# Second sequence's causal triangle: zeroed in the exponentials by POOL and VectorE instead of masked by TensorE products

## The chip, the cores and the metric

The kernel runs on one core of one Trainium2 chip. The metric is the device time of one execution in microseconds (us). Engines are called by the profile's names: PE is TensorE, ACT ScalarE, DVE VectorE, POOL GpSimd, and SP starts most DMAs.

## What is computed

Two sequences of 512 rows by 128 features go through a cross attention, a block of causal self attention and a mixture of four experts, a second cross attention, and a small feed-forward net. The change touches the causal self attention alone:

```python
scores = jnp.einsum('bqhd,bkhd->bhqk', q, k) / jnp.sqrt(jnp.float32(D))
causal = jnp.tril(jnp.ones((T, T), dtype=bool))
scores = jnp.where(causal, scores, jnp.float32(-1e+30))
p = jax.nn.softmax(scores, axis=-1)
y = jnp.einsum('bhqk,bkhd->bqhd', p, v).reshape(B, T, C)
```

There are 16 heads of 8 features (T is 512, B is 2 here). Weights of keys that lie after the query must come out as zero.

## The kernel before

The self attention runs in 32 steps s, 16 for each sequence (s = 0 to 15 the first, 16 to 31 the second). A step is four heads and one tile of 128 keys (kt = s % 4), against all queries from that tile on, so its width w is 512, 384, 256 and 128 columns for kt 0 to 3. The heads of a step are handled as pair 0 and pair 1. In a step, in this order on their engines:

- PE computes the scores of pair 0 and of pair 1, transposed (keys on partitions), into PSUM banks 0 to 3. Each pair waits for the exponential of the same pair in step s - 1, which frees its banks (`st_exp`).
- ACT takes the exponential of each pair into the SBUF buffer `PTb`, which has room for two steps: it waits until PE has used what was written two steps before (`av_step`).
- PE computes `outputs(s - 1)` (four products with the values, 32 columns of weights each) after the scores of step s. It reads `PTb`.
- In steps up to 21 PE also computes three "ring" scores each step, of which DVE takes the row maxima (`ring_maximum`, line 882, tile `mB`); two banks are used in turn, so PE and DVE wait for each other there.

Only the first 128 columns of a step lie across the diagonal and need the triangle set to nothing. In the first sequence POOL does it in the exponentials (an affine select, two heads at a time, semaphore `st_masked`, line 606). In the second sequence PE adds a constant -1e30 triangle to the scores: a product of the identity `identb` with `mask_kq`, of tile `cstb`, behind each of the four score products of a step.

The queues are in the order in which the code is written; nothing reorders them. Work of other stages is put between the steps at fixed step numbers. Those that matter here:

- DVE: `copy_outputs` (line 890) empties the bank in which the outputs of four steps gather; it stands first in step s when s % 4 is 1, and PE's first `outputs` of the next four steps waits for it (`yg_ready`). `normalise_group` follows at s % 4 == 2. `add_attention` and `ln_m` are at step 20, `route(0)` (lines 937 to 951) at step 23, `weigh_last` (lines 983, 984, nine instructions) at step 24, `place_rows(0)` (lines 958 to 977) at step 25.
- POOL: `split_maxima(c)` (lines 566 to 572) splits the maxima of a chunk of heads; PE's `turn_maxima(c)` and the later steps' scores wait for it. Chunk 7 is split after `ln_rsqrt("m")` (line 516) and `apply_m(0)` (line 616) of the next stage, and PE turns it at the end of step 23. Then POOL scatters the rows to the experts' slots, as soon as `place_rows(0)` is done.
- PE: `turn_normalised(0)` at step 18, `project_outputs(0)` at 19, `turn_sums(0)` at 21, `logits(0)` at 22, `rank_rows(0)` at 24, a product for `cb_mm` at 26. After step 31: `outputs(31)`, `turn_slots(0, ...)` and the experts' products.
- ACT: steps 27 to 31 also carry `load_experts(0)` and `copy_weights` of the first experts (0.6 us each).

Of the kernel before, what the change touches and what calls it, by code (L numbers as in the profile page):

```python
# [23 lines left out]
ALU = mybir.AluOpType  # L24
# [3 lines left out]
P = 128  # L28
B, T, D = 2, 512, 128
# [18 lines left out]
LEAST = -3.0e38  # L48
# [45 lines left out]
def program(nc, t_in, out):  # L94
    ctx = ExitStack()
    with ctx:
        def sb(name, shape, dt=F32):
            return ctx.enter_context(nc.sbuf_tensor(name, shape, dt))

        def sem(name):  # L100
            return ctx.enter_context(nc.semaphore(name))
# [10 lines left out]
        cst = sb("cst", [P, 3, P])  # L112
# [16 lines left out]
        mB = sb("mB", [P, B, HB, QT])  # L129
        mp = sb("mp", [P, 2, 3, HG * QT], BF16)  # L130
        mr = sb("mr", [P, HG * QT])
        nm3 = sb("nm3", [3 * HG * QT, 2, P], BF16)
        rB = sb("rB", [P, 2, HB])
        lg = sb("lg", [P, 4, NT, E])
# [181 lines left out]
        stack_ready = [[sem(f"stack_ready{b}_{g}") for g in range(HB // HG)] for b in range(B)]  # L316
        ones_ready = sem("ones_ready")
        s_mm, s_max = sem("s_mm"), sem("s_max")
        s1_mm, s1_max = sem("s1_mm"), sem("s1_max")
        m_part, m_turned, m_copied = sem("m_part"), sem("m_turned"), sem("m_copied")  # L320
        m_ready = [sem(f"m_ready{r}") for r in range(2)]
# [52 lines left out]
        M_CHUNK = 2 * HG  # L374
        N_CHUNK = B * HB // HG
        S_CHUNK = (None, 0, 3, 7, 11, 15, 20, 23)
        S_SPLIT = {2: 2, 6: 3, 10: 4, 14: 5}
        S_VAUG = 2
        S_TAIL = 18
        S_LN = 21  # L380
# [31 lines left out]
            return 6 if part else LN_BANK  # L412

        ident = cst[:, 0, :]
        identb, mask_qk, mask_kq = cstb[:, 0, :], cstb[:, 1, :], cstb[:, 2, :]
        block = ctx.enter_context(nc.Block())


# [83 lines left out]
        def _(pool):  # L502
# [53 lines left out]
            def split_maxima(c):  # L556

                b, g = divmod(c, HB // HG)
                m = mB[:, b, HG * g:HG * g + HG, :].rearrange("p h t -> p (h t)")
                pool.wait_ge(s_max, min(M_CHUNK * (c + 1), M0))  # L560
                if c >= 2:
                    pool.wait_ge(s1_max, ring_done(c))
                    pool.wait_ge(m_turned, c - 1)
                if c:
                    pool.wait_ge(m_part, 3 * c)
                pool.tensor_copy(mp[:, c % 2, 0], m).then_inc(m_part, 1)
                pool.wait_ge(m_part, 3 * c + 1)
                pool.tensor_tensor(mr[:], m, mp[:, c % 2, 0], ALU.subtract).then_inc(part_step, 1)
                pool.wait_ge(part_step, c + 2)
                pool.tensor_copy(mp[:, c % 2, 1], mr[:]).then_inc(m_part, 1)  # L570
                pool.wait_ge(m_part, 3 * c + 2)
                pool.tensor_tensor(mp[:, c % 2, 2], mr[:], mp[:, c % 2, 1], ALU.subtract).then_inc(m_part, 1)
# [26 lines left out]
                    pool.indirect_dma_start(XN[:, QT * b + t, :], None, scr_y[b],  # L599
                                            bass.IndirectOffsetOnAxis(ap=pos[:, b, t:t + 1], axis=0)).then_inc(gathered[b], 16)  # L600

            for n in range(2 * 16):
                s, pair = divmod(n, 2)
                slot = 4 * ((s + 1) % 2) + 2 * pair
                pool.wait_ge(st_exp, n + 1)
                pool.affine_select(PTb[:, slot:slot + 2, 0:P], PTb[:, slot:slot + 2, 0:P], [[0, 2], [1, P]], ALU.is_ge, 0.0,  # L606
                                   base=0, channel_multiplier=-1).then_inc(st_masked, 1)
                if pair and s in S_SPLIT:
                    split_maxima(S_SPLIT[s])
            split_maxima(6)  # L610

            def apply_m(b):
                pool.wait_ge(ln_rstd["m"], b + 1)
# [33 lines left out]
        def _(dve):  # L647
# [146 lines left out]
                dve.tensor_copy(cstb[:], cst[:]).then_inc(consts_ready, 1)  # L794

            def row_biases():
                own(dve.tensor_copy(rowbias[:], maskx[:]))
                own.wait()
                own(dve.tensor_scalar(rowbias[:], rowbias[:], -1.0, 1.0, ALU.mult, ALU.add))
                own.wait()  # L800
                own(dve.tensor_scalar(rowbias[:], rowbias[:], -MASK_NEG, None, ALU.mult))
# [210 lines left out]

            for m in range(M0):
                maximum(m)
            for s in range(2 * 16):
                g = (s - 5) // QT
                if s % QT == 1 and s >= 5:
                    copy_outputs(*divmod(g, 4))
                if s < M_STEPS:
                    ring_maximum(3 * s)  # L1020
                if s % QT == 2 and s >= 6 and not 4 <= g < 5:
                    normalise_group(*divmod(g, 4))
                if s == 1:
                    weigh_router()
                elif s == 3:
                    centre_router()
                elif s == S_TAIL + 2:
                    add_attention(0)
                    ln_m(0)
                elif s == S_TAIL + 5:  # L1030
                    route(0)
                    normalise_group(1, 0)
                elif s == S_RANK:
                    weigh_last()
                elif s == S_RANK + 1:
                    place_rows(0)
                elif s == S_CB + 1:
                    bias_last()
                if s < M_STEPS:
                    ring_maximum(3 * s + 1)  # L1040
                    ring_maximum(3 * s + 2)
            copy_outputs(1, 3)
            normalise_group(1, 3)
            add_attention(1)
# [331 lines left out]
        def _(pe):  # L1376
            def mm(o, lhsT, rhs, start=True, stop=True):
                return pe.matmul(o, lhsT, rhs, start=start, stop=stop)  # L1378
# [285 lines left out]
            def outputs(s):  # L1664

                bg, kt = divmod(s, QT)
                b, g = divmod(bg, 4)
                if s < 16:
                    pe.wait_ge(st_masked, 2 * s + 2)
                else:  # L1670
                    pe.wait_ge(st_exp, 2 * s + 2)
                if s == 0:
                    pe.wait_ge(v_ready, 3)
                    pe.wait_ge(preC_act, N_PREC)
                elif s == 16:
                    pe.wait_ge(v_ready, 3 * B)

                if kt == 0 and bg:
                    pe.wait_ge(yg_ready, bg)
                for j in range(4):  # L1680
                    i = mm(PS[32 * j:32 * j + 32, AV_BANK, kt * P:T], vaug[:, b, kt, 4 * g + j, :],
                           PTb[:, 4 * ((s + 1) % 2) + j, 0:T - kt * P], start=kt == 0, stop=kt == QT - 1)
                i.then_inc(av_step, 1)
# [79 lines left out]
            for s in range(2 * 16):  # L1763
# [7 lines left out]
                for pair in range(2):  # L1771
                    if s >= 1:
                        pe.wait_ge(st_exp, 2 * (s - 1) + pair + 1)
                    else:
                        pe.wait_ge(s_max, M0 - 2 + pair)
                    for j in range(2):
                        h = 4 * g + 2 * pair + j
                        o = PS[:, 2 * pair + j, 0:w]
                        i = mm(o, ks[b][:, h, kt * P:kt * P + P], qs[b][:, h, kt * P:T], stop=b == 0)
                        if b:  # L1780
                            i = mm(o[:, 0:P], identb, mask_kq, start=False)
                    i.then_inc(st_mm, 1)
                    if s < M_STEPS:
                        ring_scores(3 * s + pair)
# [225 lines left out]
```

## Time and profile before

| | |
|---|---|
| time, median of 3 runs | 346.1 us (345.12 to 346.39) |
| the profiled execution's own time | 344.6 us |
| its span in the trace | 342.7 us |
| PE busy | 319.4 us, 93% of the span |
| DVE busy | 240.8 us, 70% |
| ACT busy | 216.5 us, 63% |
| POOL busy | 127.6 us, 37% |

The page of the profile gives each engine's busy time, the granted clock of PE, and the chain of work that ended last, of which 64% lies on PE. Busy times of PE overlap, since its products are pipelined: what one costs in a busy stretch is the distance from its start to the next start. The rows further below are start and length in us from the start of the span. In the timeline, instructions of a kind that follow each other without a gap are one row with their count.

### The profile page before, as it was taken

What the parts mean: (1) busy time and instruction counts of PE and PEld (TensorE: products, weight loads), DVE (VectorE), ACT (ScalarE), POOL (GpSimd) and SP (SyncE); (2) the same over time, 40 slices, a digit from 0 to 9 for tenths busy, and PEclk for the clock granted to TensorE, in tenths of its full rate; (3) what the DMA queues carried; (4) which work ended last, traced back from release to release, by engine and by line L of the source; (5) the groups of instructions that cost most, each with busy time, mean ns of one, the idle gap of its engine ahead of it and who ended that gap; (6) DMA issues with size and microseconds to landing.
All of it is one profiled execution on the core that took longest, in us unless ns stands there. A gap on an engine that the chain in (4) does not pass through costs nothing.

```text
span 342.7 us, 6887 instructions
## 1 busy us (share of the span) xinstructions
PE 319.4 (93%) x2398; PEld 228.1 (67%) x2398; DVE 240.8 (70%) x594; ACT 216.5 (63%) x641; POOL 127.6 (37%) x183
## 2 busy tenths in 40 slices
PE   7799989998999999999899998998999899999886
PEld 2348878664655444455544898995678687878675
DVE  4988875884776788777652463369787867888476
ACT  1388885374455756555468754754766676676995
POOL 3455563110731444310631260410695525545400
PEclk9999999999999999999999999999999999999999
DMA  7590000084852430073002003200200000000002
GB/s 209 187 282 7 2 0 2 10 273 137 237 187 70 118 95 1 3 288 83 4 18 71 2 23 91 59 0 1 55 17 17 0 2 0 4 0 0 2 0 63
DMA packets 21880, 22.47 MB, mean 66 GB/s; under 512 B 3894, under 2 KB 18646, under 8 KB 21846
## 3 DMA queue, kind: packets, MB, share of 16 engines
q1 hardware_dynamic: 18982, 16.78, 16.8%
q10 hardware_dynamic: 2352, 4.20, 3.6%
q0 software_dynamic: 512, 1.05, 1.0%
q8 instruction: 20, 0.33, 0.4%
q14 instruction: 14, 0.11, 0.1%
HBM read 14.22 MB, written 7.60 MB: 64 GB/s over the span
## 4 chain that ended last, share of the span: by engine, by line
PE 64%; ACT 13%; DVE 12%; issue 4%; POOL 4%; DMA 3%; ACTq 0%; POOLq 0%; DVEq 0%
PE PS L1378 57%; PE PS L1432 5%; ACT big L1166 5%; ACT big L1354 3%; POOL big L528 2%; DVE big L690 2%; DVE big L715 2%; DMA X<-in_x 1%; PE PS L1695 1%; DMA XN<-scr_y,pos 1%; DVE mB L882 1%; DVE stats L656 1%; DVE XN L667 1%; ACT big L1140 1%; POOL big L530 1%
## 5 line engine op out<-in xcount | busy, mean ns | idle before, releaser
L1378 PE MATMUL PS<-big 128*128 128x128 f32 (+10 forms) x592 | 95.6, 308 | 6.6 <-DVE mB L882 2.3
L1378 PEld LDWEIGHTS PS<-big 128*128 128x128 f32 (+3 forms) x592 | 58.3, 150 | 34.7 <-issue 11.3
L528 POOL TENSOR_TENSOR big<-big,urec 128x1024 f32<-128x1024 f32 x24 | 45.6, 1898 | 59.9 <-DVE urec L722 45.5
L1166 ACT ACTIVATE big<-big 128x154 f32<-128x154 f32 x192 | 60.5, 318 | 10.1 <-DVE big L690 5.0
L1296 ACT ACTIVATE big<-PS 128x1024 f32<-128x1024 f32 (+3 forms) x64 | 42.9, 702 | 30.2 <-PE PS L1378 30.1
L1140 ACT ACTIVATE big<-PS 128x1280 f32<-128x1280 f32 (+2 forms) x30 | 32.3, 1087 | 27.0 <-PE PS L1432 24.5
L882 DVE TENSOR_REDUCE mB<-PS 128x2 f32<-128x256 f32 (+2 forms) x66 | 38.6, 600 | 11.9 <-PE PS L1378 11.6
L1378 PE MATMUL PS<-kkC,XT 128*128 128x462 f32 (+1 forms) x96 | 36.0, 511 | 1.9 <-DVE big L715 1.9
L1378 PE MATMUL PS<-cstb 128*128 128x128 bf16 x192 | 37.5, 220 | 0.0
L516 POOL TENSOR_TENSOR rstd<-ve,minus_half 128x4 f32<-128x4 f32 (+2 forms) x13 | 13.2, 1016 | 63.4 <-DVE ve L662 63.4
L1166 ACT ACTIVATION_READ_ACCUMULATOR big<-big 128x1 f32 x192 | 36.1, 188 | 0.0
L1378 PEld LDWEIGHTS PS<-vwCm,big 128*128 128x128 f32 x256 | 30.9, 192 | 3.9 <-ACT big L1140 1.3
L1432 PE MATMUL PS<-cst,big 128*128 128x128 f32 x240 | 30.6, 275 | 2.4 <-POOL big L530 1.8
L1378 PE MATMUL PS<-vwCm,big 128*128 128x128 f32 x256 | 31.3, 276 | 1.0 <-DVE X L745 0.5
L704 DVE TENSOR_REDUCE mraw<-PS 128x3 f32<-128x462 f32 (+1 forms) x48 | 26.0, 579 | 7.2 <-PE PS L1378 5.8
L1432 PEld LDWEIGHTS PS<-cst,big 128*128 128x128 f32 x240 | 26.6, 141 | 6.4 <-POOL big L530 6.2
L715 DVE SCALAR_TENSOR_TENSOR big<-PS,rowbias,umax 128x462 f32<-128x462 f32 (+1 forms) x48 | 27.5, 629 | 0.0
L1378 PEld LDWEIGHTS PS<-kkC,XT 128*128 128x128 f32 x96 | 17.0, 190 | 15.0 <-issue 11.9
L1378 PE MATMUL PS<-big,cw 128*32 128x512 f32 (+3 forms) x256 | 23.8, 444 | 0.3
L1378 PE MATMUL PS<-cw 128*32 128x128 f32 (+2 forms) x128 | 22.5, 351 | 0.8 <-ACT vwCm L1140 0.7
L606 POOL TENSOR_SCALAR_AFFINE_SELECT big<-big 128x256 f32<-128x256 f32 x32 | 12.9, 408 | 24.2 <-ACT big L1296 23.9
L1378 PEld LDWEIGHTS PS<-cstb 128*128 128x128 bf16 x192 | 18.9, 98 | 3.2 <-issue 1.6
(191 smaller groups left out, 508.1 us busy)
## 6 DMA issues: line engine op xcount, KB each, us to landing
scr_qk<-big SPq DMA_DIRECT2D x12, 384.0 KB, 3.4
big<-scr_qk SPq DMA_DIRECT2D x16, 288.0 KB
big<-in_wv ACTq DMA_DIRECT2D x1, 2048.0 KB, 7.9
scr_x<-zrow SPq DMA_DIRECT2D x2, 448.0 KB, 7.0
scr_y<-big SPq DMA_DIRECT2D x2, 448.0 KB, 3.9
X<-in_x ACTq DMA_DIRECT2D x2, 256.0 KB, 4.0
big<-in_A_WoT ACTq DMA_DIRECT2D x1, 512.0 KB, 5.0
cw<-in_C_Wk SPq DMA_DIRECT2D x1, 512.0 KB, 4.7
```

The costliest lines, as they stand in the source:

```text
L516: pool.tensor_tensor(rstd[:, s], ve[:, s], minus_half[:, s], ALU.pow).then_inc(ln_rstd[name], 1)
L528: pool.tensor_tensor(pn[:, 0:GH * P].rearrange("p (h k) -> p h k", h=GH), Pt[u % 3][:, :, 0:KM], r.to_broadcast([P, GH, KM]), ALU.mult).th ...
L606: pool.affine_select(PTb[:, slot:slot + 2, 0:P], PTb[:, slot:slot + 2, 0:P], [[0, 2], [1, P]], ALU.is_ge, 0.0, base=0, channel_multiplier= ...
L704: own(dve.tensor_reduce(mraw[:, u % 2, h0:h1], s, AX.X, ALU.max))
L715: dve.scalar_tensor_tensor(Pt[u % 3][:, h0:h1, :], s, bias(u), umax[:, u % 2, h0:h1].unsqueeze(2).to_broadcast([P, h1 - h0, KEYS]), ALU.ad ...
L882: dve.tensor_reduce(mB[:, b, h:h + len(heads), qt], PS[:, ring_bank(k), 0:len(heads) * w].rearrange("p (j w) -> p j w", w=w), AX.X, ALU.ma ...
L1140: return act.activation(dst, src, ACT.Copy, scale=scale)
L1166: i = act.activation(Pt[u % 3][:, h, :], Pt[u % 3][:, h, :], ACT.Exp, accum_out=usum[:, u % 3, h:h + 1])
L1296: act.activation(PTb[:, slot:slot + 2, 0:w], PS[:, 2 * pair:2 * pair + 2, 0:w], ACT.Exp, scale=float(HDB) ** -0.5).then_inc(st_exp, 1)
L1354: act.activation(RJ[:, j, c], sT[:, c], ACT.Relu, scale=vec[:, V_W1 + j:V_W1 + j + 1], bias=vec[:, V_B1 + j:V_B1 + j + 1]).then_inc(relu_r ...
L1378: return pe.matmul(o, lhsT, rhs, start=start, stop=stop)
L1432: i = pe.transpose(PS[:, T_BANK[st] + k // 4, (k % 4) * P:(k % 4) * P + P], PN[v % 2][:, k * P:k * P + P], ident)
```

## The change

The 64 mask products of the second sequence are gone. In steps 16 to 21 POOL's affine selects, unchanged in form, go on as in the first sequence (twelve more). In steps 22 to 31 DVE takes the minimum of the exponentials with a constant tile `cut`, which is 0 where the key lies after the query and 3e38 elsewhere: two instructions a step, twenty in all, each of 128 partitions by two heads by 128 columns, float32. `outputs(s)` waits for `st_masked` up to step 21 and for `st_cut` from step 22 on. `split_maxima(6)` now stands behind the selects of step 18, and what followed it on POOL stands behind the selects of step 21. `cut` is made by one DVE instruction in the first attention (`row_biases`).

```diff
-        S_SPLIT = {2: 2, 6: 3, 10: 4, 14: 5}
+        S_SPLIT = {2: 2, 6: 3, 10: 4, 14: 5, 18: 6}
+        S_CUT = 22
...
-            for n in range(2 * 16):
+            for n in range(2 * S_CUT):
...
-            split_maxima(6)
...
             def row_biases():
+                own(dve.tensor_scalar(cut[:], cst[:, 2, :], 0.0, -LEAST, ALU.is_ge, ALU.mult))
...
+            def cut_triangle(s, pair):
+
+                slot = 4 * ((s + 1) % 2) + 2 * pair
+                dve.wait_ge(st_exp, 2 * s + pair + 1)
+                dve.tensor_tensor(PTb[:, slot:slot + 2, 0:P], PTb[:, slot:slot + 2, 0:P],
+                                  cut[:].unsqueeze(1).to_broadcast([P, 2, P]), ALU.min).then_inc(st_cut, 1)
+
             for s in range(2 * 16):
                 g = (s - 5) // QT
                 if s % QT == 1 and s >= 5:
                     copy_outputs(*divmod(g, 4))
                 if s < M_STEPS:
                     ring_maximum(3 * s)
+                if s >= S_CUT:
+                    cut_triangle(s, 0)
                 if s % QT == 2 and s >= 6 and not 4 <= g < 5:
                     normalise_group(*divmod(g, 4))
...
                 if s < M_STEPS:
                     ring_maximum(3 * s + 1)
                     ring_maximum(3 * s + 2)
+                if s >= S_CUT:
+                    cut_triangle(s, 1)
...
-                if s < 16:
+                if s < S_CUT:
                     pe.wait_ge(st_masked, 2 * s + 2)
                 else:
-                    pe.wait_ge(st_exp, 2 * s + 2)
+                    pe.wait_ge(st_cut, 2 * (s - S_CUT) + 2)
...
-                        i = mm(o, ks[b][:, h, kt * P:kt * P + P], qs[b][:, h, kt * P:T], stop=b == 0)
-                        if b:
-                            i = mm(o[:, 0:P], identb, mask_kq, start=False)
+                        i = mm(o, ks[b][:, h, kt * P:kt * P + P], qs[b][:, h, kt * P:T])
```

Three places show how the queues stand. The first is DVE's queue in steps 24 and 25. Before: the last row of `normalise_group`, `weigh_last` (`WW`, `b2r`), `copy_outputs` (`cw<-PS`), and the start and the end of `place_rows(0)`.

```order
L901 TENSOR_TENSOR cw<-PS,rB 128x4x32 [waits yT_mm,own_dve]
L983 TENSOR_SCALAR WW<-wout,vec 128x128 [waits ld_d]
L983 TENSOR_SCALAR WW<-wout,vec 128x128 x7
L984 TENSOR_SCALAR b2r<-ones,vec 64x128
L890 COPY cw<-PS 128x512 [waits y_turned,av_step]
L958 TENSOR_TENSOR over<-PS,fullk 128x16 [waits rank_mm]
...
L977 CAST pos<-posf 128x4
```

The same place in the change (the minimum with `cut` is line 1022; the pair of two rows are pair 1 of step 23 and pair 0 of step 24, then pair 1 of 24, pair 0 of 25, and pair 1 of 25 with pair 0 of 26):

```order
L904 TENSOR_TENSOR cw<-PS,rB 128x4x32 [waits yT_mm,own_dve]
L1022 TENSOR_TENSOR big<-big,cut 128x2x128 [waits st_exp] x2
L986 TENSOR_SCALAR WW<-wout,vec 128x128 [waits ld_d]
L986 TENSOR_SCALAR WW<-wout,vec 128x128 x7
L987 TENSOR_SCALAR b2r<-ones,vec 64x128
L1022 TENSOR_TENSOR big<-big,cut 128x2x128 [waits st_exp]
L893 COPY cw<-PS 128x512 [waits y_turned,av_step]
L1022 TENSOR_TENSOR big<-big,cut 128x2x128 [waits st_exp]
L961 TENSOR_TENSOR over<-PS,fullk 128x16 [waits rank_mm]
...
L980 CAST pos<-posf 128x4
L1022 TENSOR_TENSOR big<-big,cut 128x2x128 [waits st_exp] x2
```

`weigh_last` now begins only after the exponential of pair 0 of step 24, and the copy and `place_rows(0)` stand behind waits for exponentials too.

The second is POOL's queue from the second sequence's first step on. Before: the last selects of the first sequence, the split of chunk 6, then `ln_rsqrt("m")`, `apply_m(0)` and the split of chunk 7.

```order
L606 AFFINE_SELECT big<-big 128x2x128 [waits st_exp] x2
L566 CAST mp<-mB 128x16 [waits m_turned,m_part,s1_max,s_max]
...
L516 TENSOR_TENSOR rstd<-ve,minus_half 128x4 [waits ln_var_m]
L616 TENSOR_SCALAR XN<-U,mv,rstd 128x128 [waits v_ready,ln_rstd_m]
L616 TENSOR_SCALAR XN<-U,mv,rstd 128x128 x3
L566 CAST mp<-mB 128x16 [waits m_turned,m_part,s1_max,s_max]
```

In the change, from the selects up to step 18 on:

```order
L609 AFFINE_SELECT big<-big 128x2x128 [waits st_exp] x8
L569 CAST mp<-mB 128x16 [waits m_turned,m_part,s1_max,s_max]
...
L609 AFFINE_SELECT big<-big 128x2x128 [waits st_exp] x6
L519 TENSOR_TENSOR rstd<-ve,minus_half 128x4 [waits ln_var_m]
L618 TENSOR_SCALAR XN<-U,mv,rstd 128x128 [waits v_ready,ln_rstd_m]
L618 TENSOR_SCALAR XN<-U,mv,rstd 128x128 x3
L569 CAST mp<-mB 128x16 [waits m_turned,m_part,s1_max,s_max]
```

The chain that makes chunk 7 now stands behind six selects, the last of which waits for the last exponential of step 21.

The third is PE's queue at step 28 and 29, where `outputs(28)` is the row with 32x512. Before:

```order
L1378 MATMUL PS<-big 128x384 [waits st_exp]
L1378 MATMUL PS<-cstb 128x128
L1378 MATMUL PS<-big 128x384
L1378 MATMUL PS<-cstb 128x128
L1378 MATMUL PS<-big,cw 32x512 [waits yg_ready,st_exp]
L1378 MATMUL PS<-big,cw 32x512 x3
```

In the change:

```order
L1392 MATMUL PS<-big 128x384 [waits st_exp]
L1392 MATMUL PS<-big 128x384
L1392 MATMUL PS<-big,cw 32x512 [waits yg_ready,st_cut]
L1392 MATMUL PS<-big,cw 32x512 x3
```

The mask products are gone, and the outputs wait for DVE's minimum as well as for DVE's copy.

## Rows read from the trace of the kernel before

**Rows 1.** The page: granted clock of PE in 40 slices of the span.

```profile
PEclk9999999999999999999999999999999999999999
```

**Rows 2.** Windows: busy us of each engine, clock, DMA share, over steps 21 to 31.

```profile
core 0: us, PE busy (x) PEld busy (x) DVE busy (x) ACT busy (x) POOL busy (x), PEclk, DMA share, GB/s
163.00:171.00 8.00, 7.03 (x67) 4.13 (x67) 4.87 (x15) 3.26 (x8) 4.94 (x9) 1.00 0.02 5
171.00:179.00 8.00, 7.48 (x80) 3.75 (x76) 5.28 (x26) 5.07 (x8) 2.14 (x2) 1.00 0.04 11
179.00:187.00 8.00, 7.35 (x80) 3.32 (x76) 1.24 (x3) 7.31 (x13) 1.98 (x3) 1.00 0.28 84
```

**Rows 3.** Timeline, PE: first and last of eight starts, scores and masks of step 27.

```profile
178.04 0.23 PE L1378 MATMUL PS<-big 75*128 75x128 bf16 x1
...
178.46 0.22 PE L1378 MATMUL PS<-cstb 128*128 128x128 bf16 x1
```

**Rows 4.** Timeline: exponentials of steps 8, 12, 16 and 20, and the projection (step 19).

```profile
128.77 1.02 ACT L1296 ACTIVATE big<-PS 128x1024 f32<-128x1024 f32 x1 [1.92 <-PE PS L1378]
138.57 1.02 ACT L1296 ACTIVATE big<-PS 128x1024 f32<-128x1024 f32 x1 [1.92 <-PE PS L1378]
148.48 1.02 ACT L1296 ACTIVATE big<-PS 128x1024 f32<-128x1024 f32 x1 [1.83 <-PE PS L1378]
...
158.03 1.11 PE L1378 MATMUL PS<-projw,cw 128*128 128x128 f32 x8
...
159.73 1.94 ACT L1296 ACTIVATE big<-PS 128x1024 f32<-128x1024 f32 x2 [2.03 <-PE PS L1378]
```

**Rows 5.** Page and timeline: POOL's selects, its chain to chunk 7, `turn_maxima(7)`.

```profile
L606 POOL TENSOR_SCALAR_AFFINE_SELECT big<-big 128x256 f32<-128x256 f32 x32 | 12.9, 408 | 24.2 <-ACT big L1296 23.9
...
162.59 1.39 POOL L516 TENSOR_TENSOR rstd<-ve,minus_half 128x4 f32<-128x4 f32 x1 [7.65 <-DVE ve L662]
...
164.77 0.81 ACT L1296 ACTIVATE big<-PS 128x768 f32<-128x768 f32 x1 [1.55 <-PE PS L1378]
...
168.18 0.22 POOL L572 TENSOR_TENSOR mp<-mr,mp 128x16 bf16<-128x16 f32 x1
...
170.96 0.24 PE L1378 MATMUL PS<-cstb,mp 128*48 128x128 bf16 x1
```

**Rows 6.** Timeline of steps 24 and 25: DVE, the exponential (24, 0), outputs 24, 25.

```profile
171.36 1.65 DVE L983 TENSOR_SCALAR WW<-wout,vec 128x128 f32<-128x128 f32 x8
...
171.89 1.02 ACT L1296 ACTIVATE big<-PS 128x1024 f32<-128x1024 f32 x1 [0.97 <-PE PS L1378]
...
173.12 0.67 DVE L890 COPY cw<-PS 128x512 f32<-128x512 f32 x1
...
173.72 0.15 DVE L958 TENSOR_TENSOR over<-PS,fullk 128x16 f32<-128x16 f32 x1
...
174.57 1.06 PE L1378 MATMUL PS<-big,cw 128*32 128x512 f32 x8
...
175.52 0.16 DVE L977 CAST pos<-posf 128x4 int32<-128x4 f32 x1
...
176.84 0.85 PE L1378 MATMUL PS<-big,cw 128*32 128x384 f32 x8
```

**Rows 7.** Timeline of steps 28 to 31: exponentials, outputs 28, outputs 30 and 31.

```profile
180.15 1.93 ACT L1296 ACTIVATE big<-PS 128x1024 f32<-128x1024 f32 x2
...
182.68 1.07 PE L1378 MATMUL PS<-big,cw 128*32 128x512 f32 x8
...
186.20 0.66 ACT L1296 ACTIVATE big<-PS 128x256 f32<-128x256 f32 x2
186.29 1.04 PE L1378 MATMUL PS<-big,cw 128*32 128x256 f32 x16
```

**Rows 8.** Timeline and page: a DVE operation on two SBUF tiles; POOL's line 516.

```profile
337.13 0.42 DVE L1105 TENSOR_TENSOR big<-big 128x256 f32<-128x256 f32 x1
...
L516 POOL TENSOR_TENSOR rstd<-ve,minus_half 128x4 f32<-128x4 f32 (+2 forms) x13 | 13.2, 1016 | 63.4 <-DVE ve L662 63.4
```

More of the change, by code:

```diff
@@ L131, in program @@
         mr = sb("mr", [P, HG * QT])
+        cut = sb("cut", [P, P])
         nm3 = sb("nm3", [3 * HG * QT, 2, P], BF16)
@@ L318, in program @@
         s_mm, s_max = sem("s_mm"), sem("s_max")
+        st_cut = sem("st_cut")
         s1_mm, s1_max = sem("s1_mm"), sem("s1_max")
@@ L414, in program @@
         ident = cst[:, 0, :]
-        identb, mask_qk, mask_kq = cstb[:, 0, :], cstb[:, 1, :], cstb[:, 2, :]
+        identb, mask_qk = cstb[:, 0, :], cstb[:, 1, :]
         block = ctx.enter_context(nc.Block())
```

## The prediction

> **What bounds the kernel now.** I read the page first, then the windows over the causal attention of the second sequence, then the timeline of all engines there. PE is at its full clock of 2.4 GHz in every slice [rows 1]. In the windows from 163 to 187 us PE is busy 7.0 to 7.5 us of every 8, ACT is light at first and has 7.31 of 8 us in the last one, DVE falls from 5.28 to 1.24 [rows 2]. So three things take turns: up to step 21 PE and DVE's row maxima, in steps 22 to 26 PE, in steps 27 to 31 ACT, which there carries 0.6 us weight copies between its exponentials. What comes after (the experts, the second cross attention) starts behind `outputs(31)`, so a delay there is a delay at the end.
>
> **What the 64 mask products cost.** Their duration (0.22 us) is no price, since they overlap. In step 27 eight products, score and mask in turn, start between 178.04 and 178.46 us [rows 3]: seven distances of 0.06 us. So 64 of them hold PE's queue for 3.8 us: 24 up to step 21 (1.4 us) and 40 in steps 22 to 31 (2.4 us).
>
> Not all of it is on the path. From exponential (8, 0) to (12, 0) four steps with POOL's selects took 138.57 - 128.77 = 9.80 us, from (16, 0) to (20, 0) four steps with masks took 159.73 - 148.48 = 11.25 us [rows 4]. The masks would be 0.96 us of the 1.45 between, but the projection is 1.11 us of it [rows 4] and four transposes come on top. So part of the added work filled PE's waits for DVE's maxima, and part of what is taken away will turn into such waits. Before exponential (21, 1) the gain lies between 0 and 1.4 us; I take 0.8, a bit over the middle, since the longest run of PE work here, step 19, gives back all of its masks.
>
> **Where that gain goes: POOL.** A select takes 0.41 us [rows 5] and in the first sequence it is hidden by the ring scores between exponential and outputs; so it is in steps 16 to 20. But the chain that makes chunk 7 now waits for the last select of step 21. Before, it ran from 162.59 (`rstd`) to 168.18 + 0.22 = 168.40, 5.81 us, and `turn_maxima(7)` started at 170.96, 2.5 us later, without waiting [rows 5]. Now exponential (21, 1), before at 164.77 + 0.81 = 165.58, ends 0.8 earlier at 164.78; 0.05 for the semaphore and 0.41 for the select give 165.24, a semaphore and 5.81 more 171.1, and PE turns the chunk at 171.2. That is 0.25 after its time before, with all gains gone: PE waits there some 1.4 us (0.8 and the 0.5 us of masks of steps 22 and 23). Behind it are the scores of step 24; two masks fewer ahead of exponential (24, 0) leave it 0.1 late: 172.0, end 173.0.
>
> **Then DVE.** No row shows the minimum itself. It reads two SBUF tiles and 256 elements a partition; that form took 0.42 us [rows 8]. Below, the select's 0.41 is no other value; I bound it by the one-input instructions of half the size, eight in 1.65 us with 0.28 for one [rows 6], and above by the 0.67 of a 512-element copy [rows 6]. I take 0.42; as successive instructions overlap by 0.08 (eight of 0.28 in 1.65 us are 0.20 apart), one delays what follows on DVE by 0.34.
>
> Price by itself: twenty times 0.34 is 6.8 us on an engine that has 2.7 to 6.8 us free in 8. What counts is the order. Steps 24 and 25, from exponential (24, 0) at 173.0:
> - minimum (24, 0): 173.05 to 173.4; `weigh_last` behind it. Before it began at 171.36, in DVE's idle time, and held it until the copy at 173.12: 1.76 us [rows 6]. Now until 175.15.
> - minimum (24, 1): 0.34, then `copy_outputs(1, 1)`, 0.67: ends 176.2. `outputs(24)` waits for both. A semaphore and weight load of 0.15: 176.3 against 174.57 [rows 6]: 1.75 late.
> - minimum (25, 0) 176.1 to 176.4; `place_rows(0)`, before from 173.72 to 175.52 + 0.16, 1.96 us [rows 6]: until 178.4; minimum (25, 1) until 178.8. `outputs(25)` at 178.9 against 176.84 [rows 6]: 2.1 late.
>
> Queued behind on PE are the scores of step 27, less two masks: exponential (27, 0) is 1.95 late. From there on ACT is the bound and keeps the lag; its `load_experts(0)` needs `place_rows(0)` at 178.4, in time. The masks taken from steps 27 to 31 buy nothing there.
>
> **Step 28** has the same form, small. Exponential (28, 1) ended at 180.15 + 1.93 = 182.08 and `outputs(28)` began at 182.68 [rows 7]. Now 182.08 + 1.95 = 184.03, minimum and copy behind each other, 0.05 + 0.34 + 0.67 + 0.15: 185.25, 2.55 late. Exponentials (30, 0) to (31, 1) are 2.45 late. The last ended at 186.20 + 0.66 = 186.86, and `outputs(31)`, the second half of the sixteen products from 186.29 on [rows 7], began at about 186.8. Now 189.3 + 0.05 + 0.42 + 0.1 = 189.9: 3.0 late.
>
> **Small terms.** `cut` is built in the first attention: at most the 0.28 us of a one-input instruction, I take nothing to 0.1. Later selects on POOL cost nothing: POOL scatters only after `place_rows(0)`, whose 2.7 us of delay (178.4 for 175.68) stay under that of `outputs(31)`, so the loads of the slots stay hidden. My gain of 0.8 cannot come back, POOL's chain eats it; but `rstd` took 1.39 us against a mean of 1.02 [rows 5, 8], and if it takes 1.02 all after it is up to 0.37 earlier. I take half: 3.0 becomes 2.8.
>
> **Sum:** 2.8 us on the profiled execution's 344.6 gives 347.4; on the median of 346.1, which lies 1.5 above it, 348.9 us, 0.8% slower. 0.5% (1.7 us) is about what a measurement of this kernel can tell from no change.
>
> **A rule on POOL's port.** `rstd`'s longest instance, 1.39 us [rows 5], is the one that ran beside a DVE addition of two SBUF tiles (`x_plus_u`). The Trainium skill, GPSIMD Engine Reference, section 1 (Specifications), says that POOL shares its SBUF interfaces with VectorE and is slowed by instructions with two SBUF inputs. The minimum is one. By it the two minima of step 22 stretch `apply_m(0)`; the sum would be 0.4 us more, 349.3.
>
> **Rivals.**
> - *Faster, PE's relief survives.* What is queued on DVE in steps 24 and 25 fits into its idle time, 2.7 us in 8 [rows 2], and PE, not the other queues, sets the pace up to step 26. The gain would be up to 1.4 up to step 21 and 1.2 for the twenty masks of steps 22 to 26, before ACT is the bound, less 0.5 at `outputs(31)`: 2.1, so 344.0. It decides at `outputs(24)`: it came 1.6 us after the end of exponential (24, 0), and the DVE chain ahead of it, which adds up to 3.2, would have to be shorter than that. Chance 0.09.
> - *Little change.* The gain before step 21 is 1.4 and `rstd` takes 1.02, so POOL's chain ends 1.0 earlier, and a minimum takes 0.28, six of them on the path (24 and 25 twice, 28, 31): 0.8 less. Of 3.0 remain 1.2: 347.3. Chance 0.25.
> - *Port contention.* Each minimum and each POOL instruction beside it is slower: minima of 0.67 add 0.25 six times, with the 0.4 above: 350.8. For it speaks the one long `rstd`; against it that POOL is idle in steps 24 and 25, waiting for `place_rows(0)`. Chance 0.12.
> - *PE's clock falls.* With waits of 1.4, 1.8 and 1 us within 8 us PE may go to 1.2 GHz for some us; 3 us of products in steps 25 to 27 would take 6: 351.9. The Trainium skill (TensorE: Matmul & The Clock Gate, "What's actually happening") says that activity releases the throttle and idling restores it. Against it: clock 1.00 in the window in which PE was busy least, 7.03 of 8 us [rows 2]. Chance 0.04.
>
> The forecast itself has 0.50. Range 346.4 to 351.0: below it lies the faster case and an edge of the second (0.12 together), above it the clock case and an edge of contention (0.07). The forecast's own range is 347.9 to 349.9. Faster by over 0.5%: 0.08. Within: 0.01 of the faster case, 0.20 of the second, 0.05 of the forecast. Slower: the rest, 0.66.
>
> **What the changed kernel's profile would show.** No `cstb` product within the second sequence's score quartets. PE waiting over 1 us before `turn_maxima(7)`, released by POOL. `outputs(24)` and `outputs(25)` released by DVE, 1.5 to 2 us later than before, with `weigh_last` starting only after exponential (24, 0). ACT without idle time from (27, 1) to (29, 1). `outputs(31)` waiting 0.5 us for DVE. A minimum of 0.42 us. I am wrong if `outputs(24)` starts by 175, if the lag shrinks in steps 27 to 31, or if the lag at `turn_slots` does not arrive at the end.

## The result and the profile after

The changed kernel takes 349.9 us (median of 4 runs, 349.73 to 350.04) against 346.2 (4 runs, 345.12 to 346.39): 1.0115 times as long, with an interval of 1.0098 to 1.0133. The forecast was 348.9. Direction and size are near, but the profile shows that only a part of the loss has the reasons given.

First the page of the changed kernel (its profiled run took 349.8 us): busy time of each engine, then the granted clock of PE in 40 slices.

```profile
span 347.7 us, 6792 instructions
...
PE 320.8 (92%) x2334; PEld 225.2 (65%) x2334; DVE 248.7 (72%) x615; ACT 216.3 (62%) x641; POOL 132.7 (38%) x195
...
PEclk9999999999999999998769999999999999999999
```

PE has 64 products fewer (2334 for 2398) and is busy 1.4 us longer (319.4 before). The last row says why: where [rows 1] has a 9 in each slice there is now 8, 7, 6. The windows put it in time (us of busy time in 3, count, then the clock as a share of 2.4 GHz):

```profile
core 0: us, PE busy (x) PEld busy (x) DVE busy (x) ACT busy (x) POOL busy (x), PEclk, DMA share, GB/s
...
159.00:162.00 3.00, 1.57 (x17) 0.55 (x15) 2.86 (x12) 2.23 (x4) 1.29 (x3) 1.00 0.00 0
162.00:165.00 3.00, 2.52 (x10) 0.88 (x14) 2.64 (x5) 0.81 (x1) 0.36 (x1) 0.50 0.03 7
165.00:168.00 3.00, 3.00 (x17) 1.48 (x10) 0.69 (x1) 0.00 (x0) 2.89 (x5) 0.50 0.00 0
168.00:171.00 3.00, 3.00 (x27) 1.79 (x24) 0.91 (x2) 1.57 (x3) 2.25 (x6) 0.86 0.00 0
171.00:174.00 3.00, 1.89 (x16) 0.56 (x13) 2.29 (x12) 1.74 (x5) 0.00 (x0) 1.00 0.00 0
174.00:177.00 3.00, 1.45 (x17) 0.51 (x17) 3.00 (x13) 2.52 (x4) 0.00 (x0) 0.77 0.04 11
177.00:180.00 3.00, 2.76 (x12) 1.08 (x13) 2.43 (x14) 0.00 (x0) 0.00 (x0) 0.50 0.01 1
180.00:183.00 3.00, 3.00 (x19) 1.09 (x17) 1.22 (x4) 1.08 (x2) 2.21 (x3) 0.59 0.06 22
183.00:186.00 3.00, 2.40 (x25) 0.70 (x24) 1.14 (x4) 2.33 (x5) 1.91 (x2) 1.00 0.19 66
```

There are two stretches at 1.2 GHz (0.50). Ahead of each PE did little: 1.57 of 3 us from 159 to 162, 1.45 of 3 from 174 to 177. [Rows 1] has a 9 in every slice there, and [rows 2], from 163 on, 1.00. The timeline names the waits (start, length, instruction, then the idle time before it and what ended it):

```profile
162.48 0.50 PE L1392 MATMUL PS<-big 72*128 72x384 bf16 x1 [1.91 <-DVE mB L885]
...
163.76 0.81 ACT L1310 ACTIVATE big<-PS 128x768 f32<-128x768 f32 x1 [2.19 <-PE PS L1392]
164.19 1.94 PE L1392 MATMUL PS<-big,cw 128*32 128x512 f32 x8
164.64 0.41 POOL L609 TENSOR_SCALAR_AFFINE_SELECT big<-big 128x256 f32<-128x256 f32 x1 [2.68 <-ACT big L1310]
165.01 1.01 POOL L519 TENSOR_TENSOR rstd<-ve,minus_half 128x4 f32<-128x4 f32 x1
...
172.13 0.22 PE L1392 MATMUL PS<-cstb,mp 128*48 128x128 bf16 x1 [0.43 <-DVE lg L940]
...
172.92 1.02 ACT L1310 ACTIVATE big<-PS 128x1024 f32<-128x1024 f32 x1 [1.21 <-PE PS L1392]
...
174.32 1.65 DVE L986 TENSOR_SCALAR WW<-wout,vec 128x128 f32<-128x128 f32 x8
...
176.08 0.41 DVE L1022 TENSOR_TENSOR big<-big,cut 128x256 f32<-128x256 f32 x1
176.42 0.67 DVE L893 COPY cw<-PS 128x512 f32<-128x512 f32 x1
...
177.24 1.93 PE L1392 MATMUL PS<-big,cw 128*32 128x512 f32 x8 [1.68 <-DVE cw L893]
...
179.15 0.16 DVE L980 CAST pos<-posf 128x4 int32<-128x4 f32 x1
```

The first fall follows a wait of 1.91 us for DVE's ring maximum in step 21. In [rows 5, 6] the same work runs at full speed; here eight products of 512 columns take 1.94 us (1.06 in [rows 6]), so PE is at half its clock from about 162 to 169. `turn_maxima(7)` starts at 172.13 and not at 170.96. DVE's chain of steps 23 to 25 then stands as forecast: `weigh_last` only behind the minimum of pair 0 of step 24, a minimum and the copy behind it, and `outputs(24)` at 177.24, 2.67 us after [rows 6]. PE waits 1.68 us for it, and its clock is at 1.2 GHz again. `outputs(25)` is at 181.00, 4.16 after [rows 6]; it waits for nobody, PE itself is late.

At the end of the stretch the row of `outputs(30)` and `outputs(31)` begins with a wait for a minimum:

```profile
191.84 1.21 PE L1392 MATMUL PS<-big,cw 128*32 128x256 f32 x16 [0.51 <-DVE big L1022]
```

The 0.51 us stand ahead of `outputs(30)`. `outputs(31)`, for which a wait of 0.5 us was forecast, starts at 192.62, 0.15 us after PE was done with `outputs(30)`. The minima, all twenty, by line: shortest, median and longest in ns, and who waited for it.

```profile
L1022 DVE TENSOR_TENSOR big<-big,cut x20: 404/424/482, 168.7 to 192.2; 128x256 f32<-128x256 f32 x20
...
  PEld PS L1392: 6.1, 6
  PE PS L1392: 1.3, 2
```

It takes 0.42 us, the value taken.

### The profile page after: what moved, and what is told of

Same layout as the page of the kernel before. It is cut to its first block, busy times and chain, and to the rows that moved or that the text cites. A ratio compares the mean times of both kernels' runs of the same rounds, so it can differ in the third digit from the quotient of the medians.

```text
span 347.7 us, 6792 instructions
## 1 busy us (share of the span) xinstructions
PE 320.8 (92%) x2334; PEld 225.2 (65%) x2334; DVE 248.7 (72%) x615; ACT 216.3 (62%) x641; POOL 132.7 (38%) x195
## 4 chain that ended last, share of the span: by engine, by line
PE 66%; DVE 13%; ACT 12%; issue 4%; POOL 3%; DMA 1%; SPq 0%; ACTq 0%; POOLq 0%; DVEq 0%
PE PS L1392 58%; PE PS L1446 5%; ACT big L1180 4%; ACT big L1368 3%; DVE big L717 2%; POOL big L531 2%; DMA big<-in_A_WkT 1%; DVE big L692 1%; PE PS L1709 1%; DVE mB L885 1%; ACT big L1154 1%; DVE mraw L706 1%; DVE mraw L682 1%; ACT cw L1154 1%; DVE stats L658 1%
## 5 line engine op out<-in xcount | busy, mean ns | idle before, releaser
L1392 PEld LDWEIGHTS PS<-big 128*128 128x128 f32 (+3 forms) x592 | 57.3, 151 | 36.3 <-issue 13.6
L609 POOL TENSOR_SCALAR_AFFINE_SELECT big<-big 128x256 f32<-128x256 f32 x44 | 17.9, 409 | 36.9 <-ACT big L1310 36.5
L1392 PE MATMUL PS<-big,cw 128*32 128x512 f32 (+3 forms) x256 | 26.4, 486 | 4.1 <-DVE cw L893 2.3
L1392 PE MATMUL PS<-cstb 128*128 128x128 bf16 x128 | 25.9, 222 | 0.0
L875 DVE TENSOR_REDUCE mB<-PS 128x2 f32<-128x256 f32 (+3 forms) x20 | 16.0, 823 | 6.1 <-PE PS L1392 6.1
```

The source lines that it names most:

```text
L875: dve.tensor_reduce(mB[:, 0, 2 * hp:2 * hp + 2, qt], PS[:, bank:bank + 2, 0:(qt + 1) * P], AX.X, ALU.max, negate=True).then_inc(s_max, 1)
```

## The experiments

The time of the kernel before was taken beside each. Its mean granted clock is known for each run: of 51 runs 15 had 1.000 (343.24 to 345.24 us, median 344.6) and 36 had 0.989 to 0.995 (344.78 to 347.33, median 346.1). The profiled run behind the rows of before (344.6 us, clock 1.000) is of the first kind. The four runs of the changed kernel all had 0.98.

### The two parts apart

**e1_pool_only:** selects by POOL in steps 16 to 21, mask products from step 22 on, no minimum.

```diff
-                if s >= S_CUT:
-                    cut_triangle(s, 0)
...
-                if s >= S_CUT:
-                    cut_triangle(s, 1)
...
-                    pe.wait_ge(st_cut, 2 * (s - S_CUT) + 2)
+                    pe.wait_ge(st_exp, 2 * s + 2)
...
+                        if s >= S_CUT:
+                            i = mm(o[:, 0:P], identb, mask_kq, start=False)
```

> One part alone: steps 16 to 21 by POOL's selects, steps 22 to 31 by PE's mask products as before, no minimum on DVE. Theory A (two costs in each part: a wait put into a queue, and a fall of PE's clock behind it): exponential (21, 1) 1.0 to 1.4 us earlier than before, then the clock at 0.5 for some 6 us from step 21 on and POOL's chunk 7 late, no second fall, DVE's step 24 untouched: exponential (24, 0) 0.5 to 1.6 later than before, end 347 to 348. Theory B (the fall of the clock at step 21 has nothing to do with POOL's part or is chance): clock 1.00 throughout, exponential (24, 0) within 0.3 of before, end 346 to 346.5.

**e2_dve_only:** mask products in steps 16 to 21 and POOL's queue as before, minima from step 22 on.

```diff
-            for n in range(2 * S_CUT):
+            for n in range(2 * 16):
...
+            split_maxima(6)
...
+                        if 16 <= s < S_CUT:
+                            i = mm(o[:, 0:P], identb, mask_kq, start=False)
```

> The other part alone: masks by PE in steps 16 to 21, DVE's minimum in steps 22 to 31, POOL's queue as before. Theory A: steps up to 23 as before with clock 1.00, outputs (24) 1.7 us late by DVE's queue, then the clock at 0.5 for some 7 us, outputs (31) 3.5 to 5 late, end 349 to 350.5. Theory B (the second fall of the clock follows from the first, PE being behind already): no fall, outputs (31) 2.5 to 3 late, end 348.5 to 349.

Measured: e1 343.8 us against 345.7 (0.9944, 0.9917 to 0.9971), e2 350.5 (1.0131, 1.0088 to 1.0173). So the loss is DVE's part alone, and POOL's part by itself is a gain. e2 ends as theory A had it. e1 ends 3 us below the range of theory A and 2 below that of B: in its profiled run the clock fell, and exponential (24, 0) came 1.2 us after that of before, as A had it, but that run took 344.95 us and the other five 342.8 to 344.0. Probably A's end was put too high because it started from medians of before that hold a fall already (e6 below). The profiled runs of both have a fall of the clock at step 21; this is one window of e1, then of e2:

```profile
165.00:168.00 3.00, 3.00 (x18) 1.50 (x11) 0.69 (x1) 0.00 (x0) 2.89 (x5) 0.50 0.00 0
```

```profile
165.00:168.00 3.00, 3.00 (x16) 0.64 (x14) 1.06 (x3) 0.81 (x1) 2.19 (x3) 0.57 0.03 6
```

e2 has the mask products there and waits 1.66 us in step 21, as the kernel before does (1.67), and falls too. So the first fall belongs to the wait in step 21, which the kernel before has as well, and not to the missing masks. The second fall (0.64 in e2 from 177 to 180) is not in e1, whose clock is 1.00 from 171 on: it comes with DVE's part. e2 has a third one, 0.85 from 186 to 189 and 0.59 from 189 to 192, which neither e1 nor the changed kernel's profiled run has.

### PE kept busy in its waits

If the clock is the part that was missed, products that do nothing, put where PE waits anyway, bring it back. They write to a bank that is free there. `hold_part` (bank, column, count) issues products of 384 columns of ones.

**e3_hold:** the changed kernel with ten of them in step 21 and nine ahead of `outputs(24)`.

```diff
+                    if s == 21 and pair == 0:
+                        pe.wait_ge(st_exp, 2 * 20 + 2)
+                        hold_part(2, 0, 10)
...
+                if s == 25:
+                    hold_part(5, 0, 9)
```

> The changed kernel with dummy products of PE in two waits: ten (384 columns, bf16, 0.16 us each) ahead of the ring score of step 21 that waits for DVE's maximum, nine ahead of outputs (24). Theory A: clock 1.00 in both stretches; the queue waits stay (chunk 7 by POOL, outputs (24) by DVE); exponential (22, 0) 0.8 earlier than before, outputs (24) 1.5 to 2 later, outputs (31) 2.5 to 3.3 later than before, end 347.8 to 348.9, some 1.5 to 2.5 us below the changed kernel. Theory B (the clock's falls lie under waits for the other engines and cost nothing): clock 1.00 but the end within 0.5 us of 349.9.

**e4_cuts_last:** the changed kernel with both minima at the end of a step on DVE, behind the rest of the step's work; no products added.

```diff
-                if s >= S_CUT:
-                    cut_triangle(s, 0)
...
                 if s >= S_CUT:
+                    cut_triangle(s, 0)
                     cut_triangle(s, 1)
```

> The changed kernel with one edit in DVE's queue: both minima of a step at the end of the step, so that route(0), weigh_last and place_rows(0) run before them, in DVE's idle time. Theory A: weigh_last runs before exponential (24, 0) ends, outputs (24) is held by minimum and copy alone and starts 1.2 to 1.7 us earlier than in the changed kernel; the first fall of the clock stays, the second is shorter or gone; end 346.5 to 348.5. Theory B (DVE's order matters little, the clock set by the mere lack of mask products is the cause): both falls stay and the end is within 0.5 us of 349.9.

Measured: e3 348.0 (347.18 to 351.74; 1.0088, 1.0043 to 1.0134), e4 348.8 (347.82 to 351.65; 1.0103, 1.0044 to 1.0163). Neither settled it. In e3 the fall in step 21 was gone, and PE then waited for POOL as forecast, where its clock fell instead:

```profile
170.80 0.30 PE L1392 MATMUL PS<-cstb,mp 128*48 128x128 bf16 x1 [1.19 <-POOL mp L575]
```

From there on e3 is at half its clock, and the nine products ahead of `outputs(24)` took 2.98 us where e5 below has 1.63. They ended at 177.84, when DVE's copy had been ready since 176.28, so here they held `outputs(24)` up themselves:

```profile
174.86 2.98 PE L1392 MATMUL PS<-onesb 128*128 128x384 bf16 x9
```

e4 has `outputs(24)` 1.17 us earlier than the changed kernel, since `weigh_last` no longer waits for an exponential, but both falls remain, the second one shorter (0.66 from 177 to 180 for 0.50), and a third is there (0.50 from 186 to 189). Its 348.8 lies 0.3 above the range of theory A.

**e5_hold_all:** the changed kernel with the products in every such wait (10, 7, 4, 9 and 4).

```diff
+                    if s == 21 and pair == 0:
+                        pe.wait_ge(st_exp, 2 * 20 + 2)
+                        hold_part(2, 0, 10)
...
+                if s == 24:
+                    hold_part(5, 0, 4)
+                elif s == 25:
+                    hold_part(5, 0, 9)
+                elif s == 26:
+                    pe.wait_ge(y_norm, 5)
+                    hold_part(6, 0, 4)
...
+                if s == 23:
+                    hold_part(5, 0, 7)
```

> The changed kernel with dummy products in all of PE's long waits: ten at step 21, seven ahead of turn_maxima(7), four ahead of outputs (23), nine ahead of (24), four ahead of (25). If the first run's account holds (queue waits of 2.8 us by the prediction's sum, and the clock's fall on top): clock 1.00 throughout, outputs (24) 1.5 to 2 us later and outputs (31) 2.5 to 3 us later than before, end 2.3 to 3 us above the runs of before that kept their clock (344.5), 346.8 to 347.5. If the clock's fall only fills waits: within 0.5 us of 349.9 although the clock holds.

**e6_before_hold:** the kernel before with the ten products of step 21 alone (the first three lines of that diff).

> The kernel before with ten dummy products of PE at step 21, in its 1.7 us wait for DVE's maximum, nothing else changed. Runs of before lay at 343.9 to 344.7 us with the clock at 1.000 and at 345.7 to 346.3 with 0.989 to 0.995. If it is the fall behind that wait that parts them: all runs with clock 1.000 at 344.0 to 344.9, median 1.2 us under that of before. If the fall is elsewhere: both kinds of run remain.

Measured: e5 347.4 (10 runs, 346.67 to 348.23; 1.0042, 1.0018 to 1.0066); six of its runs had a clock of 0.999 or 1.000 and a median of 347.04. e6 343.7 (10 runs, 343.02 to 343.99, clock 0.998 to 1.000; 0.9935, 0.9912 to 0.9959), more than the 1.2 us expected. The ten products of e6 and the product behind them:

```profile
161.38 1.79 PE L1378 MATMUL PS<-onesb 128*128 128x384 bf16 x10
163.21 0.34 PE L1378 MATMUL PS<-big 72*128 72x384 bf16 x1
```

The waits in the timeline of e5, filled:

```profile
169.26 1.31 PE L1392 MATMUL PS<-onesb 128*128 128x384 bf16 x7
170.52 0.24 PE L1392 MATMUL PS<-cstb,mp 128*48 128x128 bf16 x1
...
173.81 1.63 PE L1392 MATMUL PS<-onesb 128*128 128x384 bf16 x9
175.65 1.06 PE L1392 MATMUL PS<-big,cw 128*32 128x512 f32 x8 [0.22 <-DVE cw L893]
```

and the windows over both places of the falls:

```profile
162.00:165.00 3.00, 2.57 (x19) 0.83 (x18) 2.62 (x5) 0.81 (x1) 0.84 (x3) 1.00 0.03 7
...
174.00:177.00 3.00, 2.78 (x20) 1.19 (x19) 2.86 (x13) 0.84 (x2) 0.00 (x0) 1.00 0.02 3
177.00:180.00 3.00, 3.00 (x29) 1.64 (x31) 2.19 (x11) 1.24 (x3) 1.24 (x1) 1.00 0.00 0
...
186.00:189.00 3.00, 3.00 (x17) 1.17 (x16) 1.13 (x4) 1.60 (x3) 0.00 (x0) 0.50 0.54 158
```

Up to 183 the clock holds. e5 and e6 are then the two kernels with the clock out of the comparison, and their starts can be subtracted. (The kernels reach the causal attention some tenths apart: by exponential (8, 0) e6 is 0.67 ahead of the profile of before, e5 0.49, the changed kernel 0.56. This is not taken out of the table, which so is good to about 0.2.)

| start, us | e6 | after − e6 | e5 − e6 | forecast |
|---|---|---|---|---|
| exponential (21, 1) | 164.09 | −0.33 | −0.78 | −0.8 |
| exponential (24, 0) | 171.21 | +1.71 | +0.12 | +0.1 |
| `outputs(24)` | 173.90 | +3.34 | +1.75 | +1.75 |
| `outputs(25)` | 176.16 | +4.84 | +2.17 | +2.1 |
| exponential (27, 0) | 177.80 | +5.38 | +2.05 | +1.95 |
| `outputs(28)` | 182.01 | +5.98 | +2.65 | +2.55 |
| exponential (30, 0) | 184.04 | +5.86 | +3.17 | +2.45 |
| `outputs(31)` | 186.24 | +6.38 | +4.35 | +3.0 |
| end | 341.41 | +6.29 | +4.28 | |

Up to `outputs(28)` the queues cost what was forecast, within 0.1 us at each step, which is closer than the table can tell. At `outputs(25)` some 0.2 us are the added products' own: the minimum it waits for ended at 178.05, and it started behind them at 178.33. The last rows of e5 − e6 hold a late fall of the clock in e5's profiled run (0.95 from 183 to 186, 0.50 from 186 to 189, above). That fall follows no wait longer than 0.65 us. That run took 347.8, the six at full clock 347.04: without that fall the queues cost 347.04 − 343.67 = 3.4 us, with the added products' 0.2 in it.

### Where POOL's gain goes, and the order on DVE

**e7_pool_hold:** e1 with the ten products of step 21.

> POOL's part alone (as e1) with ten dummy products at step 21. If its gain is real and the fall at step 21 hid part of it: clock 1.000 in all runs, exponential (22, 0) 1.2 us earlier than before, chunk 7 on time to within 0.3 us, so most of the gain is lost again to POOL's chain; end 342.8 to 344.0. If the gain of e1 is chance: within 0.5 us of e6.

**e8_order_hold:** the whole change, with DVE's order mended: both minima at the end of the step, `copy_outputs` of steps 25 and 29 ahead of the minima of steps 24 and 28. Ten products in step 21, seven ahead of `turn_maxima(7)`, one each ahead of `outputs(23)` to `outputs(25)`.

```diff
-                if s % QT == 1 and s >= 5:
+                if s % QT == 1 and s >= 5 and s not in (25, 29):
...
-                if s >= S_CUT:
-                    cut_triangle(s, 0)
...
+                if s in (24, 28):
+                    copy_outputs(*divmod((s - 4) // QT, 4))
                 if s >= S_CUT:
+                    cut_triangle(s, 0)
                     cut_triangle(s, 1)
```

> The whole change with DVE's queue mended: route(0), weigh_last and place_rows(0) ahead of both minima of their step, the copies of steps 25 and 29 ahead of the minima of 24 and 28; dummy products at step 21 (ten), ahead of turn_maxima(7) (seven) and one each ahead of outputs (23) to (25). If DVE's order is what costs: outputs (24) within 0.5 us of before, outputs (25) 0.5 to 1.3 late, outputs (28) no later than exponential (28, 1) plus 0.9, outputs (31) 0.5 to 1.5 late, end 344.5 to 346. If the minimum itself costs wherever it stands: outputs (31) over 2.3 us late, end above 346.5.

Measured: e7 343.3 (8 runs, 343.12 to 343.58, clock 0.998 to 1.000; 0.9923, 0.9897 to 0.9948), 0.4 below e6. e8 345.1 (10 runs, 343.9 to 346.15; 0.9978, 0.9949 to 1.0007); its five runs at a clock of 0.998 or more have 344.27, 0.6 above e6, the other five 345.56 to 346.15. DVE and PE in e8, steps 24 and 25:

```profile
170.73 1.65 DVE L986 TENSOR_SCALAR WW<-wout,vec 128x128 f32<-128x128 f32 x8
...
172.50 0.67 DVE L893 COPY cw<-PS 128x512 f32<-128x512 f32 x1
173.10 0.84 DVE L1022 TENSOR_TENSOR big<-big,cut 128x256 f32<-128x256 f32 x2
...
174.13 1.07 PE L1393 MATMUL PS<-big,cw 128*32 128x512 f32 x8
```

With the same twenty minima, `outputs(24)` is 0.23 and `outputs(28)` 0.23 behind e6. So of the 3.4 us some 2.8 (347.04 − 344.27) are the order on DVE. Against e7, which has POOL's part and masks in place of the minima, these cost 1.0 us in e8's order and 3.8 in that of the change, both in runs at full clock.

The profiled run of e8 is one of the other five. Its clock falls late, in step 28, and `outputs(31)` is 2.2 us behind e6, outside the 0.5 to 1.5 expected:

```profile
180.00:183.00 3.00, 2.12 (x17) 0.54 (x20) 1.49 (x4) 3.00 (x5) 1.61 (x2) 0.85 0.13 44
183.00:186.00 3.00, 3.00 (x20) 1.44 (x16) 1.36 (x4) 1.47 (x3) 0.00 (x0) 0.58 0.50 150
```

The waits of PE ahead of it are short, two of 0.47 and 0.41 us for ACT. e6 and e7 have their mask products there and are busy 2.35 of the same 3 us, and none of their 18 runs has a clock under 0.998. So where ACT sets the pace the missing masks buy no time, as forecast, and may cost some: that they are the cause of the late fall is not shown, since no run puts products into these waits. With it, over all ten runs, the minima cost 1.8 us in e8's order (345.1 against 343.3).

In e7, where DVE has its old queue, PE still waits for POOL, with POOL's chain behind the last select:

```profile
164.38 0.41 POOL L609 TENSOR_SCALAR_AFFINE_SELECT big<-big 128x256 f32<-128x256 f32 x1 [2.15 <-ACT big L1306]
164.75 1.02 POOL L519 TENSOR_TENSOR rstd<-ve,minus_half 128x4 f32<-128x4 f32 x1
165.88 3.15 POOL L618 TENSOR_SCALAR XN<-U,mv,rstd 128x128 f32<-128x128 f32 x4
...
170.12 0.24 PE L1388 MATMUL PS<-cstb,mp 128*48 128x128 bf16 x1 [0.24 <-POOL mp L575]
```

**e9_pool20_hold:** e7 with the selects only up to step 20 (masks from step 21 on).

```diff
-        S_CUT = 22
+        S_CUT = 21
```

> POOL's selects in steps 16 to 20 only, PE's mask products from step 21 on, no minimum on DVE, ten dummy products at step 21. If in e7 the gain of POOL's part was lost to the chain of chunk 7 standing behind the last select of step 21: that chain now starts with the layer norm's variance, turn_maxima(7) does not wait, exponential (24, 0) is 0.8 to 1.2 us earlier than in e6 (after the difference of their starts), end 0.5 to 1.0 us below e6 and 0.3 to 0.6 below e7. If the gain is lost elsewhere: within 0.3 us of e7.

Measured: 342.7 (6 runs, 342.32 to 342.87, clock 0.999 to 1.000; 0.9911, 0.989 to 0.9933). It is the fastest of all and beats both kernels. POOL and PE there:

```profile
160.16 0.41 POOL L609 TENSOR_SCALAR_AFFINE_SELECT big<-big 128x256 f32<-128x256 f32 x1 [0.51 <-ACT big L1306]
161.01 1.38 POOL L519 TENSOR_TENSOR rstd<-ve,minus_half 128x4 f32<-128x4 f32 x1 [0.45 <-DVE ve L664]
162.50 3.14 POOL L618 TENSOR_SCALAR XN<-U,mv,rstd 128x128 f32<-128x128 f32 x4
...
169.37 0.24 PE L1388 MATMUL PS<-cstb,mp 128*48 128x128 bf16 x1
```

The chain starts at 161.01 as soon as DVE has its operand, `turn_maxima(7)` no longer waits, exponential (24, 0) is at 170.30, 0.91 before that of e6, and the span ends 0.85 before it. The medians are 342.7 and 343.7. e9 was timed apart from e6, beside runs of before with a median of 345.5 and not 345.9, so its gain is 0.8 to 1.0 us.

## Why the prediction was right and where it was wrong

**Right, the chain of queues.** Each forecast that rests on an order (the table above) is confirmed up to `outputs(28)`, once the clock is held: the gain of 0.8 ahead of exponential (21, 1), the loss of all of it at `turn_maxima(7)`, 1.75 at `outputs(24)`, 2.1 at `outputs(25)`. That the order on DVE makes most of the loss is shown by e8. e9 shows POOL's part of the theory: without the two selects of step 21 ahead of the chain the gain is kept. The 0.8 itself was a choice between 0 and 1.4, and its closeness is in part luck.

**The clock's rival was given too little: the step that failed.** It had 0.04, "against it: clock 1.00 in the window in which PE was busy least, 7.03 of 8 us". That was one execution, and the window was too wide and began too late: in windows of 3 us the same trace of before has

```profile
162.00:165.00 3.00, 1.33 (x10) 0.58 (x8) 2.93 (x10) 1.20 (x3) 2.30 (x3) 1.00 0.01 1
```

with the wait of 1.67 us for the ring maximum in it. In 36 of 51 runs of this kernel the clock is below 1, and e6, which fills that one wait, has none under 0.998. So the 1.5 us between the profiled run (344.6) and the median (346.1), which the forecast added as something outside the trace, was this fall at step 21, for the most part (see Open). In the changed kernel all four runs have the clock of the profiled one, 0.98, with its two falls, and by e5 they cost 349.88 − 347.04 = 2.8 us. In the traces the first fall makes the changed kernel 2.2 us later than e5 at exponential (22, 0) and 1.6 at `turn_maxima(7)`, since PE then arrives when the chunk is ready and does not wait 1.2 us for it as in e3; the second adds 1.7 by exponential (27, 0). Of these 3.3 us 2.8 are found in the times; where the rest goes is not shown.

**Why the number was near all the same.** With its waits filled the kernel before takes 343.67 us and the changed one, at full clock, 347.04, so 3.4 for the queues where the sum had 2.8. From there to the medians before has 2.6 more (346.2) and after 2.8 (349.9). The sum took the median with its fall as a base, so it had one fall in it without knowing, and the changed kernel's two falls happened to cost about as much. That was luck: on the profiled execution's 344.6, the base without a fall, the same sum gave 347.4, 2.5 us too little. The miss of 1.0 us is 0.6 of queues, 0.3 of what lies between full clock and median, and 0.1 of the base, whose fourth run moved its median.

**The term that was a bit small.** The forecast had 3.0 at `outputs(31)` and took off 0.2 for `rstd`. That was half right: `rstd` took 1.01 us as hoped, 0.38 less than in [rows 5]. But in e5 the four instructions of `apply_m(0)` took 3.64 us, in e7, without minima beside them, 3.15: the two that had a minimum beside them took 1.03 and 1.04 us, the others 0.79 and 0.80. The rule on POOL's port had priced it: by the Trainium skill, GPSIMD Engine Reference, section 1 (Specifications), POOL is slowed beside VectorE instructions with two SBUF inputs, and these two runs agree, with 0.5 us. The changed kernel itself agrees in part: its four took 3.14, the last of them 0.78 with a minimum beside it, but a cast behind them took 0.39 beside the next minimum, for 0.20 in e7. `turn_maxima(7)` is 0.4 later in e5 than in e7 (170.52 for 170.12). The rival of contention as a whole is refuted, since the minimum itself took 0.42 (at most 0.48) and not 0.67. How the rest of the 3.4 spreads over steps 29 to 31 is not shown, because the profiled run of e5 has its late fall there.

**Signs named beforehand.** "PE waiting over 1 us before `turn_maxima(7)`, released by POOL" did not appear in the changed kernel (0.43 us, for DVE), and did in e3 (1.19, for POOL). "ACT without idle time from (27, 1) to (29, 1)" held but for 0.49 us ahead of (27, 1), which the kernel before has too; the lag does not shrink there. "`outputs(24)` and `outputs(25)` released by DVE, 1.5 to 2 us later" was half right: 2.67 and 4.16 us, and `outputs(25)` was not waiting. "`outputs(31)` waiting 0.5 us for DVE" did not appear in the changed kernel (0.15) and did in e5 (0.59). "The lag at `turn_slots` does not arrive at the end" was to prove it wrong: against e6 it arrives (6.4 at `outputs(31)`, 6.3 at the end). Against the profile of before 0.7 is missing, and 0.5 of it lies in before: its chain of waits has a gather's transfer of 3.87 us late in the kernel, e6 has it with 3.40.

**Little change** (0.25) was refuted by 1.0098 as the lower bound, as was the faster case. Little change needed a minimum of 0.28 us (0.42 measured) and a gain of 1.4 before step 21 (0.8); the faster case a shorter chain on DVE at `outputs(24)`. e8, in which that chain is shorter but the clock is held in part by added products, has 0.9978 (0.9949 to 1.0007).

**Open.** Why the kernel before falls in some runs and not in others with the same wait is not settled, and no run here tells from which length a wait does it. The 0.5 us between before's runs at full clock (344.2 beside e6) and e6 itself isn't explained in full; the gather's 0.47 would be of that size, but was seen in one run of each. What a fall costs the kernel before differs between the three groups of its runs: 2.0 us (344.2 to 346.2), 1.5 (344.6 to 346.1) and 0.7 (345.2 to 345.9). And the late falls of e2, e4, e5 and e8 are seen but not explained.

## What to carry to other kernels

Price moved work by what stands behind it in its new queue and when that is wanted, not by its busy time: twenty minima of 0.42 us in place of masks cost 1.0 us in one order and 3.8 in another (at full clock), and selects on an idle engine were worth 0.8 to 1.0 us or 0.4, without or with the two that stand ahead of a chain others wait for. Before a profile is used as the base, compare its clock and its time with the other runs: here it was like the 15 of 51 runs with a full clock, and the wait in step 21 that looked harmless in it cost the others 1.6 us by the medians (346.1 against 344.6). Where PE must wait for a microsecond or two, products without a use in the wait are worth a try; ten of them alone made the kernel before 0.65% faster (e6). They have to end before the wait does: in e3, at half clock, they did not.

## What was unexpected of the hardware

- The clock fell to 1.2 GHz behind waits of 1.9 us (step 21) and 1.7 us (ahead of `outputs(24)`), in e3 behind one of 1.19 us, in e5 with no wait over 0.65 us from 180 on, and in e8 behind two of 0.47 and 0.41. The changed kernel's profiled run has a wait of 0.65 us too, ahead of `outputs(28)`, and keeps 1.00 behind it. The Trainium skill (TensorE: Matmul & The Clock Gate, "What's actually happening") says that activity releases the throttle and idling restores it; these runs agree in kind, and no run here tells how long a wait has to be.
- The same kernel with the same queues shows it in some executions only: a clock below 1.000 in 36 of 51 runs of the kernel before, 0.98 in 4 of 4 of the changed one, nothing below 0.998 in the 10 of e6.
- Products without a use cost nothing that could be measured while they end before the wait does: in e6 ten took 1.79 us in a wait of 1.67, from 161.38 on, and the product behind them started at 163.21, 0.68 ahead of the profile of before like everything around it.
- A minimum reading a tile that is broadcast over two heads takes the same 0.42 us as one on two full tiles [rows 8].
